# Layer 1 of a decoder: the eight experts' shares are spread over partitions by DMA instead of by selector matmuls

## The reference

```python
def _fused_branch(Q_side, K_side, V, W, U, b, ...):
    xV = jnp.einsum('btd,kdr->btkr', Q_side, V)
    yW = jnp.einsum('btd,kdr->btkr', K_side, W)
    cum_yW = jnp.cumsum(yW, axis=1)
    prod = xV * cum_yW                                # 8 experts x rank 64 for each token
    h = jax.nn.gelu(Q_side @ router_w1.T + router_b1, approximate=False)
    logits = h @ router_w2.T + router_b2 + expert_bias
    weights = jax.nn.softmax(logits, axis=-1)         # the shares: 8 numbers for each token
    out = jnp.einsum('btkr,kdr->btd', prod * weights[..., None], U)
    out = out + weights @ b
    return out / n_valid[None, :, None]
out = fwd + alpha_bi * inv
return out @ W_O.T
```

## Time and profile before

| | |
|---|---|
| median of three runs | 2461.85 us (2459.59 to 2467.96) |
| the profiled execution's own time | 2476.02 us |
| span of its profile | 2474.2 us |
| mean granted TensorE clock | 0.91 of full speed |
| PE busy | 2145.5 us (87%) |
| DVE busy | 1319.0 us (53%) |
| ACT busy | 1001.1 us (40%) |
| POOL busy | 382.4 us (15%) |

### The profile page before, as it was taken

One profiled execution on the slowest core, in us unless ns is written; L12 is line 12 of the kernel. 1 busy time (PEld: TensorE's weight loads), 2 busy tenths in 40 slices (PEclk: granted clock), 3 DMA queues, 4 the chain that ended last, 5 costly groups with the idle time before them and its releaser, 6 DMA issues. The chain is left out here.

```text
span 2474.2 us, 38944 instructions
## 1 busy us (share of the span) xinstructions
PE 2145.5 (87%) x13559; PEld 1526.4 (62%) x13623; DVE 1319.0 (53%) x3911; ACT 1001.1 (40%) x3152; POOL 382.4 (15%) x655
## 2 busy tenths in 40 slices
PE   8588988998999988896638799899999999999986
PEld 4266666665777755776424566666666666666654
DVE  7235576576443464321136667666666565757442
ACT  3123555645453434451112444544444444544221
POOL 2044253362414052001000000000000000000000
PEclk9757999998998988997859899999999999999988
DMA  8000000002222112446640000000000000000000
GB/s 317 9 1 5 6 10 6 10 14 84 90 86 86 46 42 69 163 165 214 177 167 1 2 11 5 6 10 7 5 11 5 5 11 5 6 5 5 5 1 9
DMA packets 51051, 116.27 MB, mean 47 GB/s; under 512 B 8224, under 2 KB 30496, under 8 KB 47008
## 3 DMA queue, kind: packets, MB, share of 16 engines
q1 hardware_dynamic: 48880, 101.60, 12.3%
q10 hardware_dynamic: 432, 7.89, 0.9%
q0 software_dynamic: 1536, 4.20, 0.6%
HBM read 90.20 MB, written 23.46 MB: 46 GB/s over the span
## 5 line engine op out<-in xcount | busy, mean ns | idle before, releaser
L702 ACT ACTIVATE PRS<-PT 128x384 f32<-128x384 f32 (+1 forms) x512 | 266.0, 519 | 613.8 <-PE PT L633 613.7
L767 DVE TENSOR_REDUCE negmax<-SM 128x2 f32<-128x512 f32 x432 | 283.6, 685 | 199.6 <-PE SM L596 96.3
L633 PE MATMUL PT<-const_sb,PRS 128*128 128x128 f32 x1664 | 299.6, 296 | 55.9 <-ACT PRS L702 54.1
L717 ACT ACTIVATE PRS<-SM,negmax 128x128 f32<-128x128 f32 x608 | 248.2, 420 | 151.9 <-DVE negmax L767 148.1
L633 PEld LDWEIGHTS PT<-const_sb,PRS 128*128 128x128 f32 x1664 | 198.9, 149 | 149.8 <-issue 99.0
L2916 DVE TENSOR_SCALAR arena<-arena 128x256 bf16<-128x256 bf16 x1024 | 212.0, 281 | 8.9 <-PE SC L2934 7.9
L586 PE MATMUL SM<-haloU,QM 32*128 32x128 f32 (+1 forms) x1056 | 158.8, 359 | 4.4 <-ACT PRS L717 2.5
L2934 PE MATMUL SC<-arena,identb 128*128 128x256 bf16 x1024 | 138.6, 278 | 7.6 <-DVE arena L2916 7.6
L586 PEld LDWEIGHTS SM<-haloU,QM 32*128 32x128 f32 x1056 | 122.0, 205 | 17.8 <-issue 8.7
L648 PE MATMUL OA<-PRS,big 128*32 128x256 f32 (+1 forms) x1024 | 131.6, 381 | 0.9 <-ACT PRS L702 0.7
L715 ACT ACTIVATE PRS<-SM,negmax 128x256 f32<-128x256 f32 x256 | 105.3, 472 | 47.1 <-DVE negmax L767 29.6
(11 more groups left out here) (594 smaller groups left out, 4060.2 us busy)
## 6 DMA issues: line engine op xcount, KB each, us to landing
arena<-lay SPq DMA_DIRECT2D x50, 1024.0 KB, 4.9
rows<-OT SPq DMA_DIRECT2D x2, 3456.0 KB, 32.2
arena<-lay ACTq DMA_DIRECT2D x1, 5265.5 KB, 25.2
arena<-lay SPq DMA_DIRECT2D x1, 3862.0 KB, 19.5
arena<-rows SPq DMA_DIRECT2D x25, 128.0 KB, 2.5
arena<-lay SPq DMA_DIRECT2D x25, 128.0 KB, 5.0
rows<-arena SPq DMA_DIRECT2D x25, 128.0 KB, 4.3
rows<-OT SPq DMA_DIRECT2D x1, 2432.0 KB, 21.6
```

The lines of the kernel that those rows point to most:

```text
L633: ins = pe.transpose(bank[:, o:o + P], PR[n % 4][:, t, k * P:(k + 1) * P], ident)
L702: act.activation(dst, src, ACT.Copy).then_inc(S("probs_moved"), 1)
L717: ins = act.activation(dst, src, ACT.Exp, bias=negmax[:, h, r:r + 1], accum_out=rsum[:, t, h:h + 1])
L767: st.post(dve.tensor_reduce(negmax[:, ORDER[s], :], two(banks[s % NB]), AX.X, ALU.max, negate=True), S("max_ready"))
```

## The change

The two selector matmuls and their bank go away. DVE posts `weights_ready` with the copy to `WT8` and releases `bf` by a small memset. SP waits for it, writes `WT8` (16 KB) to a DRAM tensor `shares`, waits until that has landed, and reads it back with eight DMAs. Each reads one expert's row of 2 KB for 64 partitions (128 KB), into `WIDE8` (128 x 4 chunks x 2 branches x 256 tokens), which lies on the four tiles `YW` that the feed has used up by then. DVE waits for all eight in step 13 and multiplies `WIDE8` into `PD` from SBUF, two multiplications in step 13, one each in steps 14 and 15. PE has nothing in steps 12 to 15 and waits for the four multiplications ahead of the final product. SP's list is put in another order around this.

```diff
@@ -2937,6 +2939,15 @@
+        def widen_weights(sp, i):
+
+            sp.wait_ge(S("weights_ready"), i + 1)
+            sp.dma_start(shares_d[i], WT8).then_inc(S("weights_out"), 16)
+            sp.wait_ge(S("weights_out"), 16 * (i + 1))
+            for e in range(KE):
+                sp.dma_start(WIDE8[e % 2 * R:(e % 2 + 1) * R, e // 2],
+                             shares_d[i, e:e + 1].broadcast_to([R, 2, T])).then_inc(S("weights_wide"), 16)
@@ feed_pe
-            for br in range(2):
-                for j in range(2):
-                    bank = bf.claim(pe)
-                    for m in range(2):
-                        ins = pe.matmul(bank[:, m * T:(m + 1) * T], k3(w1("sel8"), 4)[0:KE, 2 * j + m, :], WT8[:, br, :],
-                                        start=True, stop=True)
-                    bf.fill(ins, "dve")
-                    yield
+            yield from idle(4)
+            pe.wait_ge(S("parts_weighted"), 4 * (i + 1))
             bank = bf.claim(pe)
@@ feed_dve
             bank = bf.take(dve, "dve")
-            bf.release(st, dve.tensor_copy(WT8.rearrange("e a t -> e (a t)"), bank[0:KE, :]), "dve")
-            st.settle()
-            yield
+            st.post(dve.tensor_copy(WT8.rearrange("e a t -> e (a t)"), bank[0:KE, :]), S("weights_ready"))
+            st.settle()
+            bf.release(st, dve.memset(gate_s[:, 18:19], 0.0), "dve")
+            yield
+            yield
+            dve.wait_ge(S("weights_wide"), 16 * KE * (i + 1))
             for br in range(2):
                 for j in range(2):
-                    bank = bf.take(dve, "dve")
-                    bf.release(st, dve.tensor_tensor(PD[br][:, 2 * j:2 * j + 2, :], two(bank), PD[br][:, 2 * j:2 * j + 2, :],
-                                                     ALU.mult), "dve")
-                    yield
+                    st.post(dve.tensor_tensor(PD[br][:, 2 * j:2 * j + 2, :], WIDE8[:, 2 * j:2 * j + 2, br, :],
+                                              PD[br][:, 2 * j:2 * j + 2, :], ALU.mult), S("parts_weighted"))
+                    if br or j:
+                        yield
@@ SP's list in layer 1
+                def fed(i):
+                    if i >= 0:
+                        widen_weights(sp, i)
+                        sp.wait_ge(S("out_ready"), TT * (i + 1))
+                        sp.dma_start(out[i + 1], OUT[:]).then_inc(S("out_done"), 16)
...
+                drawn(1)
+                opening(2)
+                for i in range(1, B):
+                    drawn(i + 1)
+                    context(i)
+                    fed(i - 3)
+                    opening(i + 2)
+                for i in range(B - 3, B):
+                    fed(i)
```

More of the change, by code:

```diff
@@ L845, in decoder @@
         rows_of = [nc.dram_tensor(f"rows{g}", ((3 * q.room + q.tiles) * P, D), F32, kind="Internal").ap() for g, q in enumerate(GROUPED)]
+        shares_d = nc.dram_tensor("shares", (B, KE, 2, T), F32, kind="Internal").ap()
         zeros = OT[:, 0, 0:D]
@@ L2292, in decoder @@
         YW = [work[:, 3588 + i * 512:4100 + i * 512].rearrange("p (k t) -> p k t", k=2) for i in range(4)]
+        WIDE8 = work[:, 3588:5636].rearrange("p (m a t) -> p m a t", m=4, a=2)
         PD = [work[:, 5636 + i * 1024:6660 + i * 1024].rearrange("p (k t) -> p k t", k=4) for i in range(2)]
@@ L3159, in _, with opening, drawn, context @@
                 sp.dma_start(CT[:], ctxT[0]).then_inc(S("ctx_in"), 16)
-                for i in range(B + 2):
-                    if i + 1 < B:
-                        sp.wait_ge(S("idx_used"), i + 1)
-                        sp.dma_start(idx_i, itok[i + 1]).then_inc(S("idx_in"), 16)
-                    if i + 2 < B:
-                        sp.wait_ge(S("x2_ready"), TT * (i + 1))
-                        sp.dma_start(X1s[i % 2][:], x4_d[i + 3]).then_inc(S(f"x_in{i % 2}"), 16)
-                    if i + 1 < B:
-                        sp.wait_ge(S("cd_ready"), i + 1)
-                        sp.dma_start(CT[:], ctxT[i + 1]).then_inc(S("ctx_in"), 16)
-                    if i >= 2:
-                        sp.wait_ge(S("out_ready"), TT * (i - 1))
-                        sp.dma_start(out[i - 1], OUT[:]).then_inc(S("out_done"), 16)
+                def opening(i):
+                    if i < B:
+                        sp.wait_ge(S("x2_ready"), TT * (i - 1))
+                        sp.dma_start(X1s[i % 2][:], x4_d[i + 1]).then_inc(S(f"x_in{i % 2}"), 16)
+                def drawn(i):
+                    if i < B:
+                        sp.wait_ge(S("idx_used"), i)
+                        sp.dma_start(idx_i, itok[i]).then_inc(S("idx_in"), 16)
+                def context(i):
+                    sp.wait_ge(S("cd_ready"), i)
+                    sp.dma_start(CT[:], ctxT[i]).then_inc(S("ctx_in"), 16)
+                def fed(i):
[12 more added lines that the diff above has]
+                    fed(i)
                 sp.wait_ge(S("feat_in"), 16 * (B + 1 - FEATURES_EARLY))
```

## The result

| | before | after |
|---|---|---|
| median of 20 runs each | 2468.52 us (2455.32 to 2490.03) | 2451.74 us (2445.69 to 2466.7) |
| ratio, 95% interval | 1 | 0.994 (0.9922 to 0.9959) |
| span of the profiled execution | 2474.2 us | 2448.8 us |
| from feed 0's copy to `WT8` to the end | 804.1 us | 788.7 us |

The account below looks back on a forecast made before the run. PE bounds where an attention runs (feeds 0 to 4), latency in feeds 5 to 7. Terms: -17.5 under cover, -1.75 without, +3.0 for the clock, -16.25; taken as 16, giving 2446 us, 8 in 10 within 2435 to 2462.

Parts of the forecast that it names:

- Under cover, 3.5 us per feed: Feeds 0 to 4: 2.1 us saved ahead of L396 plus 1.4 at L586 in each, 17.5 us in all.
- The wait under cover costs nothing: Slot 3, feeds 0 to 4: DVE's wait for the reads is hidden by 10.4 us of cover; at T = 11.0 costs 0.6.
- T = 7.5: Time from the end of the copy to `WT8` until the last of eight reads lands; 7.5 us, bounds 7.3 to 11.0.
- Without cover, 3T - 24.25 = -1.75: Feeds 5 to 7: change in when the next PE work starts after the copy, together 1.75 us earlier.
- The clock without cover, 3.0: Feeds 5 to 7: idle PE returns at a lower clock, costing 0 to 2.2 us each, 3.0 taken in all.
- The upper end of 6.6 us: Feeds 5 to 7: most the lower clock could cost in all, the case by the skill's warning of idle stretches.
- Its own signs of being wrong: Wrong if T is above 10 us, counts lengthen where tallies shorten, or PE waits for ACT in slots 2 and 3.
- Of the rivals, the first: Slots 2 and 3, feeds 0 to 4: freed PE time returns as wait; -4 us, 2458; chance 0.17.
- The second: Slot 5, feeds 0 to 4: row maxima move too, all 5.1 us per feed come; -24 us, 2438; chance 0.10.
- The third: Reads: slow at 107 KB per us, T = 13.5; +17 us, 2479, or +8, 2470, with two tight tallies; chance 0.10.
- The fourth: Reads: the eight don't overlap at all, T = 19.3; +64 us, 2526; chance 0.03.

Follow-up runs that it names:

- the split wait alone: Changed kernel, but DVE waits for the first four reads, multiplies those halves, then waits for the rest; ratio 0.9923 against the kernel before.
- the second run: Repeat, beside the changed kernel, of that kernel with reads awaited in two halves and unread matmuls on PE in feeds 5 to 7; ratio 0.991 against before.

## Why the prediction was right

Forecast and result agree: 2446 us by a loss of 16, measured 2451.74 and a ratio worth 14.8, and by the profile 15.4 from the first copy. The mechanism held under cover. That the sum came out so near is in part luck, since the covered gain was taken 2.2 us too small and two things on the other side were taken 1.0 and 1.8 too small (points 1, 4 to 6). Point by point:

1. *Under cover, 3.5 us per feed: right, a little small.* It is 3.93 at full clock, 19.7 for five feeds in place of 17.5: 2.42 ahead of L417 (2.1 forecast) and 1.51 behind (1.4). The limit behind it was named rightly: PE now waits 1.28 us for L717. The run with unread selector matmuls splits it into 3.0 of PE's time and 0.9 of the bank's hand-over.
2. *The wait under cover costs nothing: right, but with less to spare than forecast.* In feed 0 T was 9.75 us, for the most part because the write took 2.4, and 0.35 us of cover were left. Without the round trip the tally is equally long; with a second round of reads it is not.
3. *T = 7.5: mis-sized.* It is 8.6 to 8.9. The forecast took the plain issue's 0.47 us; the issue with 64 partitions, 0.60 in the earlier trace rows, was the right row (0.615), worth 1.0 in T. The landing is 2.8 in place of 2.4, and the write with SP's reaction 1.5 in place of 1.8. All lie within the bounds of 7.3 to 11.0.
4. *Without cover, 3T - 24.25 = -1.75: wrong in sign by that.* The formula itself holds: with the mean T of 8.77 it gives +2.06, and measured are 12.66 + 11.68 + 11.17 - 33.99 = +1.5.
5. *The clock without cover, 3.0: too dear.* Only feed 7 seems to have paid, 0.88 us, and even that is not shown to be the change's: with the old code there its 16 records took 5.23, 6.19 and 6.73 us in three profiles, against 6.11 and 6.02 in two of the changed kernel. Feeds 5 and 6 had the low clock before as well: 4.62 and 5.50 us for their first 16 final records now, 4.64 and 5.77 before. The upper end of 6.6 us wasn't paid. Points 4 and 5 together were forecast at +1.25 and measured at +2.26; the two errors cancelled for the most part.
6. *What the forecast had not.* In the profiled executions the counts, which nobody edited, took 6.6 us more at a lower clock, and the tallies 4.8 less than the equal-clock gain accounts for: +1.8 in all.
7. *Its own signs of being wrong.* One of the three came: the counts got longer where the tallies got shorter. The sign stood for work that only moves from a tally to a count. That isn't so: the long count has the same 507 PE records as the short one and 80.66 us of PE in place of 77.39, at 0.96 in place of 1.00, and with SP's order alone the counts are as long without a shorter tally. T stayed under 10 us wherever DVE waited for it, and in slots 2 and 3 of feed 0's tally PE's rows follow each other without a wait from 1661.41 to 1676.7. Later than the forecast's ranges came the eighth read (8.6 to 8.9 us without cover, not 7 to 8.5) and the next PE work of all three ends (12.66, 11.68 and 11.17, not 11 to 12 and twice 10 to 11).

Of the rivals, the first (PE's time comes back as a wait in slots 2 and 3) is out by the 2.42 us ahead of L417. The second needs the row maxima in slot 5 to move far enough that 5.1 us come; they moved by the 2.5 us of L417, and 3.93 came. The third is out, since T is 8.8 on average and 9.75 at most, against its 13.5 and the 11.3 from which it decides. The fourth is out, since 7 x 0.615 us of issues and one landing of 2.8 are seen, not eight landings.

## What to carry to other kernels

Work moved from the bounding engine to idle DMA queues pays where another chain covers the latency, and costs what sticks out of the cover elsewhere (here 2.6, 3.5 and 8.5 us): state the cover at each place in microseconds, and a round trip through DRAM as a sum of write, issues and landing (here 1.5 + 7 x 0.615 + 2.8). Take the issue time from a transfer of the same shape, not from the plainest row. After taking work off TensorE, read the granted clock of the stretches that were not edited, in more than one profile and in one of the old code too. Where TensorE must wait for a transfer, unread matmuls in the gap can win back a part of what the wait costs (5.5 us in one profile).

## What the runs showed of the hardware

**Unread matmuls in the tallies raised the granted clock.** The count of 80.68 us at full clock takes 83.95 at 0.96. In the changed kernel three of four whole counts were of the long kind (two of four in its second profile; four of four both with the round trip left out and with it in the covered feeds only). With the unread selector matmuls, seven of eight counts in two profiles were at 80.68. From copy to copy from feed 0's to feed 4's the mean is 127.9 us before (130.7 with SP's order alone), 125.2 and 124.4 in the changed kernel, and 126.5 and 125.7 with unread matmuls. At full clock throughout it would be 125.5, 121.6 and 124.6. So of the 3.0 us per feed in which the changed kernel should lead the unread one, some 1.3 remained in these profiles. It isn't a matter of two profiles: over all executions on which the ratios rest the mean granted clock is 0.9165 with the unread matmuls (21 executions) and 0.9095 in the changed kernel (32), which differ in those matmuls alone. Whether the change also lowered the clock against the kernel before is less clear: that has 0.912 (83 executions), but SP's order alone, with PE's old work, has 0.910 (10) and two counts of 84 us. PE's busy share in a tally falls from 0.95 to 0.93 with the change, and stays at 0.97 with the unread matmuls; that this is what the clock follows is not shown, and the kernel that reads twice speaks against it: its tallies have 0.83 to 0.85, and three of its four counts were of the short kind. Nor do the times tell the changed kernel from the unread one: the ratios are 0.994 and 0.9939 against 0.9908 and 0.9935.

**Idle gaps and the clock.** The Trainium skill (TensorE: Matmul & The Clock Gate, Why this matters for your kernels) warns of idle stretches between bursts of matmuls. By rows of this case the final product's first 16 records take 6.11 us after 11.89 us of idle PE and 3.72 with PE kept busy, and the ends of the three uncovered feeds together got shorter with it by 5.5 us against the split wait alone. The trace agrees in five of six such ends; in the sixth, feed 6 of the second run, whose unread matmuls ended 3.0 us ahead of the product, the records took 5.38 us at 0.68. In the changed kernel itself at most 0.88 us were new, since the gaps of before already had the low level.

**The same bytes kept the DMA engines busy for longer in two reads than in eight.** Eight reads, each of one 2 KB row to 64 partitions, moved 350 GB/s for the engines' busy time, as plain loads did (369), and two reads of 512 KB 224 (each kernel's one profile, feed 7). From the first to the last byte 1 MB took 5 to 6 us either way, once for the issues and once for the transfers. Both are faster than the 107 KB per us of rival 3, which was a write to DRAM beside other transfers and so the wrong row for a bound.
